# Centred down weights, one-instruction outputs and a power on GpSimd in a routed feed-forward kernel

## What is computed

```python
def _layernorm(x, axis=-1, eps=1e-05):
    m = jnp.mean(x, axis=axis, keepdims=True)
    v = jnp.var(x, axis=axis, keepdims=True)
    return (x - m) / jnp.sqrt(v + eps)
...
scores = jax.nn.sigmoid(logits) * mask                  # mask: one-hot of the largest logit
masked_inputs = scores.T[:, :, None] * x[None, :, :]
gate_up = jnp.einsum('eth,ehf->etf', masked_inputs, gate_up_proj)
gate, up = jnp.split(gate_up, 2, axis=-1)
expert_out = jnp.einsum('etf,efh->eth', up * jax.nn.silu(gate), down_proj)
shared = jax.nn.silu(x @ w_gate.T) * (x @ w_up.T) @ w_down.T
out = shared + expert_out.sum(axis=0)
...
x = x + _layernorm(_L0_ffn_ref(_layernorm(x, axis=-1), ...), axis=-1)
```

## Time and profile before

| what | value |
|---|---|
| time, median of 3 runs | 349.55 us (347.86 to 350.0) |
| profiled execution, its own time | 347.56 us |
| span of that execution | 345.8 us |
| PE busy | 264.6 us, 77% |
| DVE busy | 286.4 us, 83% |
| ACT busy | 186.6 us, 54% |
| POOL busy | 192.7 us, 56% |

### The profile page before, as it was taken

One profiled execution on the slowest core, in us unless ns is written; L12 is line 12 of the kernel. 1 busy time (PEld: TensorE's weight loads), 2 busy tenths in 40 slices (PEclk: granted clock), 3 DMA queues, 4 the chain that ended last, 5 costly groups with the idle time before them and its releaser, 6 DMA issues.

```text
span 345.8 us, 6250 instructions
## 1 busy us (share of the span) xinstructions
PE 264.6 (77%) x1465; PEld 184.2 (53%) x1465; DVE 286.4 (83%) x1138; ACT 186.6 (54%) x572; POOL 192.7 (56%) x221
## 2 busy tenths in 40 slices
PE   3459999999998995638887988821999999999000
PEld 1125556555554553325555655521999889988000
DVE  5998999999999999996998787640379999999930
ACT  2524656565665552257666664203899888885000
POOL 5056777767775863200054556570007888888870
PEclk9988999999999998967999899985899999999655
DMA  6999900000000000000011111126950101110000
GB/s 187 374 426 396 396 4 0 2 3 0 2 0 2 2 0 0 1 1 2 1 62 64 63 62 64 64 100 229 355 166 18 35 31 43 41 36 29 25 2 0
DMA packets 13668, 28.39 MB, mean 82 GB/s; under 512 B 1950, under 2 KB 10150, under 8 KB 12610
## 3 DMA queue, kind: packets, MB, share of 16 engines
q1 hardware_dynamic: 10448, 21.57, 17.1%
q0 software_dynamic: 3040, 6.37, 5.4%
q10 hardware_dynamic: 146, 0.07, 0.1%
HBM read 15.38 MB, written 13.60 MB: 84 GB/s over the span
## 4 chain that ended last, share of the span: by engine, by line
PE 39%; DVE 24%; POOL 18%; issue 12%; DMA 4%; ACT 1%; POOLq 0%; ACTq 0%; SPq 0%; another core or an unknown queue 0%; DVEq 0%
PE banks L1009 13%; POOL out L490 10%; POOL rows L484 6%; PE banks L1028 5%; PE banks L1100 5%; DVE hT L814 2%; PE banks L1037 2%; PE banks L1134 2%; POOL sorted_rows L474 2%; DVE stats L641 2%; DMA rows<-in_x 2%; PE banks L997 2%; DVE num L740 1%; DVE rows L857 1%; DVE stats L849 1%
## 5 line engine op out<-in xcount | busy, mean ns | idle before, releaser
L1009 PE MATMUL banks<-kv,upto 128*128 128x512 f32 x128 | 63.5, 621 | 1.3 <-POOL kv L449 1.3
L449 POOL TENSOR_TENSOR kv<-qk,vv 128x1024 f32<-128x1024 f32 x32 | 62.4, 1950 | 2.5
L1134 PE MATMUL banks<-xsT,w_now 128*128 128x128 f32 x376 | 52.6, 284 | 0.4 <-DVE hT_e L948 0.4
L490 POOL DMA_INDIRECT out<-rows,token_i x47 | 46.8, 997 | 9.8 <-issue 8.2
L443 POOL TENSOR_TENSOR qk<-ex,rl 128x256 f32<-128x256 f32 x32 | 23.3, 727 | 47.0 <-ACT ex L546 47.0
L1134 PEld LDWEIGHTS banks<-xsT,w_now 128*128 128x128 f32 x376 | 47.1, 197 | 1.2 <-issue 0.7
L474 POOL DMA_INDIRECT sorted_rows<-rows,slot_i x32 | 31.7, 992 | 28.7 <-DVE slot_i L804 20.7
L718 DVE TENSOR_TENSOR prod<-banks,qk 128x1024 f32<-128x1024 f32 x32 | 38.9, 1216 | 2.1 <-PE banks L1009 1.5
L740 DVE TENSOR_REDUCE num<-prod 128x128 f32<-128x1024 f32 x32 | 38.7, 1208 | 0.3 <-DVE den L735 0.3
L948 DVE TENSOR_TENSOR hT_e<-silu_e,banks 128x256 f32<-128x256 f32 x47 | 19.4, 412 | 19.8 <-ACT silu_e L623 16.1
L484 POOL TENSOR_TENSOR rows<-rows,yn 128x128 f32<-128x128 f32 x40 | 19.1, 477 | 28.0 <-DVE yn L940 26.1
(11 more groups left out here) (158 smaller groups left out, 640.0 us busy)
## 6 DMA issues: line engine op xcount, KB each, us to landing
sorted_rows<-rows SPq DMA_DIRECT2D x3, 1950.0 KB, 13.3
rows<-sorted_rows SPq DMA_DIRECT2D x11, 520.0 KB, 6.3
w_exp<-in_gate_up SPq DMA_DIRECT2D x4, 1024.0 KB, 19.7
w_exp_down<-in_down SPq DMA_DIRECT2D x4, 512.0 KB, 19.7
rows<-in_x SPq DMA_DIRECT2D x1, 1024.0 KB, 11.1
rows<-in_x SPq DMA_DIRECT2D x1, 768.0 KB, 8.4
out<-rows,token_i POOLq DMA_INDIRECT x47
sorted_rows<-rows,slot_i POOLq DMA_INDIRECT x32
```

Source lines behind the costliest of these rows:

```text
L449: nc.gpsimd.tensor_tensor(kv[:, u, :].rearrange("p (h m d) -> p h m d", h=NH, m=HD), k, v, ALU.mult).then_inc(s_kv, 1)
L490: nc.gpsimd.indirect_dma_start(out=out_rows, out_offset=bass.IndirectOffsetOnAxis(ap=token_i[:, j - 1:j], axis=0), in_=rows[:, j - 1, 0:D] ...
L1009: ins = nc.tensor.matmul(ps_s[u % 2][:, cols], upto[:], kv[:, u, cols], start=True, stop=True)
L1134: ins = nc.tensor.matmul(ps_gue[u % 2][:, c * P:(c + 1) * P], w_now[:, u % 2, c * P:(c + 1) * P], xsT[:, u % 2, :], start=True, stop=True)
```

## The change

The mean over a row's 128 values is taken out of the down weights once, instead of out of every output row. A matrix `centring` (identity minus 1/128) is made on DVE. PE multiplies the shared down weights by it in stage 1 and the experts' down weights between stages 2 and 3 (`centre`, 8 calls, 4 products each). DVE and ACT copy the results to the tiles that held the loaded weights before. Both weights arrive in the other orientation, with the same bytes. A row of the feed-forward's result then has mean zero, and its norm needs only the inverse deviation.

In stage 3, DVE makes the variances of four tiles with three small instructions, and POOL raises them to the power -0.5 with one `tensor_tensor` of op `pow`. An output is one DVE `scalar_tensor_tensor`, which multiplies by the inverse deviation and adds the residual. For every fourth tile below 40 (`OF_POOL`, ten tiles) DVE writes `yn` and POOL adds the residual. POOL also makes the token numbers. Outputs run 6 steps behind the sum instead of 8, and the last seven tiles are normed in groups of two (the last one alone).

```diff
+        centring = sb("centring", [P, P])
+        w_exp_out = sb("w_exp_out", [P, E, F])
...
+        GROUPS = [(j, j + 4) for j in range(0, 40, 4)] + [(j, min(j + 2, ST)) for j in range(40, ST, 2)]
+        OUT_LAG = [GROUPS[g][1] - GROUPS[g][0] + 2 for g in GROUP_OF]
+        OF_POOL = [j for j in range(ST) if j % 4 == 2 and j < 40]
...
+            def inverse_root3(g):
+                c = slice(*GROUPS[g])
+                pool.wait_ge(s_half, 1)
+                pool.wait_ge(s_var3, g + 1)
+                nc.gpsimd.tensor_tensor(rstd3[:, c], var3[:, c], minus_half[:, 0:c.stop - c.start], ALU.pow
+                                        ).then_inc(s_rs3, 1)
+            tokens(0)
+            inverse_root3(0)
+            for j in range(ST):
+                if j % 4 == 1 and j + 3 < ST:
+                    tokens(j // 4 + 1)
+                if j + 1 in FIRST_OF:
+                    inverse_root3(FIRST_OF[j + 1])
+                if j in OF_POOL:
+                    n = OF_POOL.index(j)
+                    x1 = flat(rows[:, j:j + 1, 0:D])
+                    pool.wait_ge(s_yn, n + 1)
+                    nc.gpsimd.tensor_tensor(x1, x1, yn[:, n % 2, :], ALU.add).then_inc(s_fin_pool, 1)
+                    pool.wait_ge(s_fin_pool, n + 1)
+                else:
+                    pool.wait_ge(s_fin, j + 1 - sum(i < j for i in OF_POOL))
+                pool.wait_ge(s_token, j // 4 + 1)
+                nc.gpsimd.indirect_dma_start(
...
+            for n in range(E // CENTRED_AT_ONCE):
+                act.wait_ge(s_turned_e, n + 1)
+                nc.scalar.copy(w_exp_down[...], ps_centred[n % 3][:]).then_inc(s_centred_e, 1)
...
+            nc.vector.tensor_tensor(centring[:], ident[:], neg_mean[:], ALU.add).then_inc(s_centring, 1)
...
+            nc.vector.tensor_copy(w_d[:].rearrange("p c d -> p (c d)"), ps_s[1][:, 0:FC * D]).then_inc(s_centred_d, 1)
...
+            def variances(g):
+                c = slice(*GROUPS[g])
+                mean_even, sq_even, sq_odd = stats3[:, c, 1], stats3[:, c, 2], stats3[:, c, 5]
+                norm.done(nc.vector.tensor_tensor(square3[:, c], mean_even, mean_even, ALU.mult))
+                norm.done(nc.vector.scalar_tensor_tensor(out=var3[:, c], in0=sq_even, scalar=D * EPS, in1=sq_odd,
+                                                         op0=ALU.add, op1=ALU.add))
+                norm.wait()
+                nc.vector.scalar_tensor_tensor(out=var3[:, c], in0=var3[:, c], scalar=1.0 / D, in1=square3[:, c],
+                                               op0=ALU.mult, op1=ALU.add).then_inc(s_var3, 1)
+            def output(i):
+                x1 = flat(rows[:, tiles(i), 0:D])
+                dve.wait_ge(s_rs3, GROUP_OF[i] + 1)
+                if i in OF_POOL:
+                    at_least(dve, s_fin_pool, n - 1)
+                    nc.vector.tensor_scalar(yn[:, n % 2, :], flat(rows[:, tiles(i), D:2 * D]), rstd3[:, i:i + 1], None,
+                                            ALU.mult).then_inc(s_yn, 1)
+                    return
+                nc.vector.scalar_tensor_tensor(out=x1, in0=flat(rows[:, tiles(i), D:2 * D]), scalar=rstd3[:, i:i + 1],
+                                               in1=x1, op0=ALU.mult, op1=ALU.add).then_inc(s_fin, 1)
...
+                for g, (j0, j1) in enumerate(GROUPS):
+                    if j == j1:
+                        variances(g)
+                while waiting and j >= waiting[0] + OUT_LAG[waiting[0]]:
+                    output(waiting.pop(0))
...
+            centre(0)
+            centre(1)
             pe.wait_ge(s_tile_rank, 1)
...
+            for n in range(2, E // CENTRED_AT_ONCE):
+                centre(n)
             pe.wait_ge(s_experts, 1)
-            pe.wait_ge(s_wexp, 16 * (E // 4) * 2)
+            pe.wait_ge(s_centred_e, E // CENTRED_AT_ONCE)
```

More of the change, by code:

```diff
@@ L390, in build @@
         ps_turn = bank[5]
+        ps_centred = [bank[2], bank[3], bank[4]]
         block = ctx.enter_context(nc.Block())
@@ L945, in step3 @@
+            waiting = list(range(ST))
+            def step3(j):
+                u = j % 4
+                if j > 0:
+                    dve.wait_ge(s_sum, min(j, ST))
                 if live(j + 2, ST):
```

141 lines of the change are left out of this document (63 added, 78 removed).

## The result

The changed kernel takes 355.95 us (median of 4 runs, 355.22 to 357.7), the kernel before beside it 349.71 us. The ratio is 1.020, with an interval from 1.014 to 1.025: slower by more than the spread of the runs, though the interval leaves open whether by more than 2%. Forecast were 341.0 us. The profiled execution took 357.70 us. Its span is 355.9 us and its last transfer starts at 346.81 us, where 328.2 was forecast; 9.1 us lie behind it, as before.

A forecast was written before the change was run, and what follows sets the result against it. The prediction took POOL's row of transfers as what ends the kernel: start 256.5 plus row 71.7 gives last transfer 328.2 instead of 336.71 us, -8.5 us, own time 339.1, median 341.0 us. The range was 335.5 to 348 us.

The forecast's parts named there:

- POOL is the bound from the first output on: Stage 3: POOL's round of four tiles takes 6.23 us, 1.56 us a tile, above PE's 1.45.
- first transfer: Start of POOL's row in stage 3: near 256.3 us, plus 0.2 for the delayed first norm, 256.5 us.
- 10 adds: POOL's adds between transfers in stage 3: each costs 0.36 us more than none, 3.6 us together.
- 11 tokens: Small token-number instructions on POOL's row, after the first: 0.20 us each, 2.2 us together.
- 13 powers: POOL's powers after the first, on its row: 0.47 us each, 6.1 us; called the least certain term.
- the power costs much: Rival: the power counts in full on POOL, 13 times; gain gone at 1.12 us, 361 at 2 us; chance 0.11.
- the band from 0.7 to 1.12 us: Middle case for one power's duration on POOL: median 344 to 349.5 us, chance 0.10.
- count of passes: Sizing of POOL's power: thirty passes over four columns, 0.27 us, plus 0.20 us start, 0.47 us; a hundred passes 1.12.
- the copy of the shared weights: DVE copy at the start, about 0.35 us: covered by DVE's 1.34 us wait for PE, otherwise 0.35 us more.
- DVE as the bound: Rival: in stage 3 DVE, waiting for power and late partners, sets about 1.6 us a tile; -5 us, 344.5; chance 0.06.
- Outputs that block POOL: Rival: 37 two-input DVE outputs hold up POOL's row 0.29 us each, 10.7 us; +2.2 us, 351.8; chance 0.05.
- The clock: Centring might keep PE's clock up before stage 3, saving nothing to 1.3 us; taken as nothing.

The follow-up runs named there:

- f1: Changed kernel with all token numbers made by one GpSimd instruction ahead of the first output, none inside the rounds: 349.84 us, ratio 1.010.
- h4: f2 with the deviations made by one GpSimd power for four tiles, two transfers ahead of the one needing it: 341.76 us, ratio 0.986.
- f3: Kernel before with only the token numbers moved to GpSimd, one small instruction for four tiles: 349.27 us, ratio 1.009.
- f4: Changed kernel with every output two tiles later behind its group's sums: 357.36 us, ratio 1.029.
- e2: Changed kernel with the token wait on POOL's add instead of on each transfer (kept on transfers of tiles 0 and 44): 356.88 us, ratio 1.022.
- i2: Changed kernel with each power earlier, ahead of the add and last but one transfer of the group before: 351.6 us, ratio 1.019.
- f2: Kernel before with centred weights, every output one DVE instruction, deviations and tokens on DVE, only transfers on POOL: 336.94 us, ratio 0.975.
- e1: Changed kernel with a product in place of the power, so the inverse deviation is not computed: 359.01 us, ratio 1.024.
- h3: Kernel of i1 with small unused DVE instructions added, so no tile's step has fewer than three: 333.38 us, ratio 0.967.
- i1: Changed kernel with deviations, outputs and tokens on DVE and only transfers on POOL, rerun unaltered on another chip: 334.47 us, ratio 0.966 (earlier 1.022).
- e3: Changed kernel with no adds on POOL, DVE writing all 47 outputs in one instruction each: 357.89 us, ratio 1.021.
- set g: Four changed-kernel variants on one chip: power earlier; that plus later outputs; deviations on DVE; also outputs and tokens on DVE. Ratios 1.041, 1.043, 1.023, 1.022.
- sets f and h: Two sets of four runs each, on one and the same chip; the kernel before took 345.2 and 345.3 us beside them.
- e4: Kernel before with the centring of both down weights and nothing else of the change: 350.11 us, ratio 1.002.

## Why the prediction was wrong

**The bound.** "POOL is the bound from the first output on" was right, as was "DVE will wait once a round for the power, and PE runs at POOL's pace". So the bound held. Two terms of its sum were far too small: a wrong size for the power, and for the add a wait that the prediction had overlooked. By the forecast's own sum, in us:

| term | forecast | measured | from |
|---|---|---|---|
| first transfer | 256.5 | 261.01 | changed kernel |
| 46 transfers at 1.30 | 59.8 | 59.3 to 59.8 | f1, h4: 1.29 to 1.30 |
| 10 adds | 3.6 (0.36 each) | 9.6 to 10.2 (0.96 to 1.02) | f1, changed kernel |
| 11 tokens | 2.2 (0.20) | 2.5 to 3.5 (0.23 to 0.32) | changed kernel, f3, f4 against f1 |
| 13 powers | 6.1 (0.47) | some 13 (9 at 1.07 to 1.2, 4 smaller) | h4, changed kernel |
| last transfer | 328.2 | 346.81 | changed kernel |
| median against the profiled execution | +2.0 | -1.75 | changed kernel |

The last line hides part of the miss: the profiled execution took 357.70 us, 18.6 more than the 339.1 forecast for it, the median only 15 us more than forecast.

**The power** is the largest miss, 7 us, and the rival "the power costs much" named it: it "counts in full, 13 times". Its own 1.07 us fall into the band from 0.7 to 1.12 us, for which the prediction had 344 to 349.5 us; by the prediction's own sum the power alone does not make the kernel slower. The step that failed is the count of passes. I took 30 passes at 2.3 ns a column; 1.06 us lies at the hundred that I put as the far end. The rows of one, two and four columns (0.60, 0.76, 1.07) show both parts off: a column adds some 0.16 us, where 30 passes made it 0.07, and what is left for the start is some 0.44 us, where the forecast had 0.20. With no row of the operation, the forecast should have stood nearer the middle of its bounds, 0.20 and 1.12.

**The add** is the second, 6 us. The step that failed was "an add costs 0.35 to 0.36 us more than none". That was the price of an add followed by the transfer of the *previous* tile, whose data had long been signalled. In the changed order the transfer behind the add is its own. It waits for the add's end, and starts 0.79 us after it instead of 0.17. The order of instructions showed this. I read only their number. e2 shows that it is not the second wait. That the 0.79 us hang on the wait for the add is argued from the two orders; the add one place earlier was not tried. The dependence alone does not explain them: in stage 2 the transfer at 214.83 us waits for the small POOL instruction just ahead of it, which writes its rows, and starts 0.36 us after that one's end. There the trace has the wait on the transfer itself. In stage 3 it stands in a record of its own on POOL's sequencer, ahead of the transfer, and the transfer starts 0.73 to 0.74 us after that record ends, behind an add (changed kernel, e2, f1, i2) as behind a wait for DVE (f2, at 284.73 us). No run tells whether another form of the wait would close the gap.

**The start.** The first `xs` of stage 3 started at 242.51 us instead of 239.31, 3.2 us later, of which the forecast had 0.2; that is 3.0 of the 4.5 us. From the end of the last scatter to that `xs` it took 7.04 us, against 5.36 before; in 15 of 16 other traces with centring it was 5.19 to 5.66 us. In the other runs with the same code ahead of stage 3, `xs` started anywhere between 234.24 (i2) and 241.96 us (e1), and centring alone changed the time by 0.2%, at most by 0.6. So I put this to the spread of executions and not to the change. At the start of stage 1 the cover of "the copy of the shared weights" seems to have failed: DVE's product began at 30.38 instead of 29.84 us, with PE ahead of it waiting 2.67 us for DVE's `carry`. That is 0.5 us, but the same product began anywhere from 29.18 to 31.46 us in the traces with centring, and at 29.24 in f3 without it, so this is not shown. The other 1.5 us lie in stage 3, most of them at the first output: the sum of tile 6 starts 0.67 us after its product, behind `hT_e` and the statistics, and POOL's transfer starts 0.86 us after the output's end, a wait of the same kind as behind the add.

**The other rivals.** DVE as the bound (344.5 us): no, it was busy for 6.68 of 10 us.

Outputs that block POOL (351.8 us): not for their whole length, but a part of it is there. In f1, h3 and h4 DVE writes two-input outputs beside transfers under way; these take 0.98 us all the same, and the output 0.34 to 0.35, or 0.54 once a round in f1 (at 295.22 us, beside a transfer of 0.98). It is otherwise where the output begins just ahead of the transfer. This one stands ahead of the transfer of 1.12 us at 297.77:

```profile
297.62 0.35 DVE L988 SCALAR_TENSOR_TENSOR rows<-rows,rstd 128x128 f32<-128x128 f32 x1 [1.26 <-POOL rstd L508]
```

In the changed kernel 17 of the 47 transfers take 1.08 to 1.13 us, and at each of them an output begins 0.08 to 0.15 us before the transfer does. Behind an add with no such output the transfer takes 0.99 to 1.00 us, in f1 and f4 every time. Behind a power, with an output that begins with the transfer and not ahead of it, it took 1.04 us (h4, at 269.67 us). So the output makes 0.07 to 0.13 us of each, together 1 to 2 us of the row, an estimate. This is the sign that the prediction had named: "transfers of more than 1.05 us beside outputs". Behind another transfer it is less: in f2, nine transfers with an output 0.16 us ahead take 1.03 to 1.04 us. Why the beginning alone is open to it, no run shows. The Trainium skill (SBUF — State Buffer, "Who interferes with whom") calls the port pair that DVE and GpSimd share an exclusive lock, for which a DVE instruction with two SBUF inputs contends; of `tensor_tensor` it adds, as inferred, that it takes only the read interface, while descriptor generation needs the write interface. These rows show neither a full block nor none.

**The clock** term, taken as nothing, was right within a microsecond. PE's last centring product ended at 236.25 us, near the forecast 236, the granted clock fell from 1.00 at 237 to 0.50 by 239 us all the same, and was back at 1.00 from 249 us, 6.5 us after the first `xs`, where before it was 245 us, 5.7 after it. From 250 to 300 us the windows stand at 1.00 before and after.

**What the change was worth without its mis-sized parts:** one-instruction outputs with all else on DVE give a ratio of 0.975 (f2) or 0.966 (i1), where late signals are absent. The power takes 1.1 points of this back (h4, 0.986). With the power and the adds, and other lags and groups, it is 1.010 (f1), with the tokens too 1.019 (i2).

## What to carry to other kernels

An engine that issues transfers is full when its list has no gap, whatever its busy share says: count distances, and put nothing on it that another engine can do. Price an instruction together with what stands behind it: the same 0.48 us add cost 0.36 us ahead of a transfer that was ready, and 0.96 us ahead of the one that waits for it. And when an edit that adds useless work makes a kernel faster, run the kernel without it again, beside the first, before believing a reason.

## What the runs showed of the hardware that I had not expected

A GpSimd power takes 1.06 us for 4 columns, 0.72 to 0.76 for 2 and 0.60 for 1. In stage 3 an indirect transfer that waits for the add just ahead starts 0.79 to 0.81 us after that one ends, and the first one of all, which waits for DVE's output, 0.86 us; in stage 2 one that waits for a small POOL instruction starts after 0.36 us. A transfer takes 0.97 to 0.99 us behind another and 0.99 to 1.04 behind an add, but 1.08 to 1.13 behind an add or a power in the changed kernel, where a DVE output begins 0.08 to 0.15 us ahead of it.

The late signals are the largest finding, and their cause is open. In e1 to e3, in all of set g, and in the profiled run of the changed kernel, the others got PE's signals up to 3.1 us late, mostly once in four tiles, while PE's records went on at their pace. In sets f and h and in i1 and i2, on three chips, there was not one over 0.4 us. The chip alone does not make them: in its one trace the kernel before has none, nor has e4, which ran on the chip of e1 to e3 and whose PE waits for others every round. They begin at full granted clock, and I found nothing in the other records that goes with them every time. Each set was also at another time, and nothing here shows whether the chip or something else that changed with the occasion makes the difference.
